# Queries and keys of one attention layer kept dimension by dimension over four heads, and copied through DRAM in that order

## What is computed

```python
qkv = (x1 @ mat_qkv_w.T + qkv_bias).reshape(B, L, 3, H, hd)      # B=16, L=256, H=16, hd=16
q, k, v = [jnp.transpose(qkv[:, :, i], (0, 2, 1, 3)) for i in range(3)]
q = _l2norm(q) * sm
k = _l2norm(k)
scores = jnp.einsum('bhqd,bhkd->bhqk', q, k)
probs = jax.nn.softmax(scores, axis=-1)
o = jnp.einsum('bhqk,bhkd->bhqd', probs, v)
```

## Time and profile before

| what | value |
|---|---|
| median of 3 runs | 795.8 us (793.74 to 796.53) |
| the profiled execution's own time | 793.83 us |
| its span, first to last instruction | 792.0 us |
| mean granted TensorE clock | 0.976 of full |
| PE busy | 731.9 us, 92% of the span |
| DVE busy | 498.2 us, 63% |
| DMA packets | 83096, 79.65 MB |

### The profile page before, as it was taken

One profiled execution on the slowest core, in us unless ns is written; L12 is line 12 of the kernel. 1 busy time (PEld: TensorE's weight loads), 2 busy tenths in 40 slices (PEclk: granted clock), 3 DMA queues, 4 the chain that ended last, 5 costly groups with the idle time before them and its releaser, 6 DMA issues.

```text
span 792.0 us, 15017 instructions
## 1 busy us (share of the span) xinstructions
PE 731.9 (92%) x4708; PEld 521.5 (66%) x4708; DVE 498.2 (63%) x1037; ACT 443.1 (56%) x733; POOL 326.1 (41%) x563
## 2 busy tenths in 40 slices
PE   4789999999996689999999999998889999999997
PEld 2477788888873345555555555555548888888885
DVE  2168999989999357767676767666425444444432
ACT  0335555555553266666666666666546555556553
POOL 1024655655653445555555555555442302222200
PEclk9999999999999599999999999999989999999999
DMA  8831333333311777776667767666500000000001
GB/s 239 292 98 37 111 94 115 115 94 113 103 32 40 126 133 149 148 147 150 146 147 146 147 147 147 146 147 155 125 14 1 22 19 14 27 27 28 14 27 40
DMA packets 83096, 79.65 MB, mean 101 GB/s; under 512 B 22942, under 2 KB 71710, under 8 KB 83054
## 3 DMA queue, kind: packets, MB, share of 16 engines
q1 hardware_dynamic: 81726, 78.95, 41.6%
q10 hardware_dynamic: 1328, 0.16, 0.1%
HBM read 57.13 MB, written 21.66 MB: 99 GB/s over the span
## 4 chain that ended last, share of the span: by engine, by line
PE 79%; ACT 6%; DVE 6%; issue 3%; DMA 1%; POOL 1%; ACTq 0%; SPq 0%; DVEq 0%; POOLq 0%
PE ps L1703 11%; PE ps L1717 11%; PE ps L1521 7%; PE ps L1439 7%; PE ps L1596 6%; PE ps L1582 6%; PE ps L1634 4%; PE ps L1531 4%; ACT probsT L928 4%; PE ps L1412 4%; PE ps L1430 4%; PE ps L1459 4%; PE ps L1470 3%; PE ps L1615 2%; PE ps L1548 1%
## 5 line engine op out<-in xcount | busy, mean ns | idle before, releaser
L928 ACT ACTIVATE probsT<-ps 128x1024 f32<-128x1024 f32 x128 | 130.5, 1019 | 29.8 <-PE ps L1582 29.5
L1331 DVE TENSOR_TENSOR hidden_low<-hidden,hidden_high 128x512 fp32r<-128x512 f32 x64 | 46.1, 721 | 115.0 <-ACT hidden_high L1024 67.1
L1021 ACT ACTIVATE hidden<-ps,b_fc 128x512 f32<-128x512 f32 x64 | 44.1, 689 | 73.5 <-PE ps L1703 72.5
L1582 PEld LDWEIGHTS ps<-q_stack,k_stack 49*128 49x128 f32 x512 | 39.0, 188 | 65.3 <-ACT probsT L928 35.3
L1582 PE MATMUL ps<-q_stack,k_stack 49*128 49x256 f32 x512 | 65.5, 335 | 11.9 <-ACT probsT L928 6.8
L1596 PE MATMUL ps<-probsT,v_ones 128*32 128x256 f32 x1024 | 69.2, 388 | 5.0 <-ACT probsT L928 4.8
L713 POOL TENSOR_TENSOR scores<-scores,row_max 128x640 f32<-128x640 f32 x32 | 42.4, 1324 | 76.2 <-DVE row_max L1060 76.2
L1225 DVE TENSOR_REDUCE neg_max<-ps 128x4 bf16<-128x344 f32 x128 | 59.5, 506 | 19.6 <-PE ps L1548 19.6
L1521 PE MATMUL ps<-w_qkv,x1T 128*128 128x512 f32 x128 | 65.3, 634 | 0.0
L1439 PE MATMUL ps<-x_res,w_q 128*128 (+1 forms) x256 | 63.7, 394 | 0.0
L1439 PEld LDWEIGHTS ps<-x_res,w_q 128*128 128x128 f32 x256 | 47.4, 194 | 11.1 <-issue 5.5
(11 more groups left out here) (181 smaller groups left out, 1714.2 us busy)
## 6 DMA issues: line engine op xcount, KB each, us to landing
parts_dram<-part_pairs SPq DMA_DIRECT2D x64, 256.0 KB
q_stack<-parts_dram SPq DMA_DIRECT2D x96, 128.0 KB, 5.3
k_stack<-parts_dram SPq DMA_DIRECT2D x96, 128.0 KB, 6.0
adj<-in_adj SPq DMA_DIRECT2D x16, 440.0 KB, 3.4
xT<-in_xT SPq DMA_DIRECT2D x16, 256.0 KB, 2.7
x_res<-in_x SPq DMA_DIRECT2D x16, 256.0 KB, 3.4
x_in<-in_x SPq DMA_DIRECT2D x16, 256.0 KB, 2.8
gate_rows<-rows_dram SPq DMA_DIRECT2D x16, 256.0 KB, 7.0
```

Source lines behind the costliest of these rows:

```text
L928: nc.scalar.activation(probsT[:, s % 4, :], ps[:, COLS:COLS + 2, :].rearrange("p a n -> p (a n)"), ACT.Exp).then_inc(exp_made, 1)
L1021: nc.scalar.activation(hidden[:, s % RAW, :], ps[:, FC1[s % FC1_BANKS], :], ACT.Gelu, bias=b_fc1[:, m:m + 1]).then_inc(gelu_made, 1)
L1331: nc.vector.tensor_tensor(hidden_parts[1][:, s % H_SLOTS, :], hidden[:, s % RAW, :], hidden_parts[0][:, s % H_SLOTS, :], ALU.subtract).the ...
L1582: mm = nc.tensor.matmul(ps[:, COLS + j, kt * N:(kt + 1) * N], k_stack[at, par, s, kt * P:(kt + 1) * P], q_stack[at, par, s, :], start=True ...
```

## The change

Within each of queries and keys the columns of SBUF are ordered by group of four heads, then dimension, then head (`g d a`, a = 4), where they were ordered by head, then dimension. PSUM, bias and weights keep the old order, so `take_qk` reads run by run and writes single elements 16 bytes apart. The sum of squares reads with the same step. `unit_qk` reads and writes in the new order, with the reciprocal roots of four heads repeated over the 16 dimensions. After the transposes a partition is (group of 4 heads, dimension, head), `parts_dram` holds [queries or keys, high or low, c, partition, token], and a dimension's four heads lie one behind the other in DRAM.

The mask `row_head` (1/3 where the partition's head is column a) follows: it is now a sum over the identity's columns, made by DVE in setup, where POOL made it from `head_of_row`.

```diff
-                    nc.gpsimd.tensor_tensor(row_head[:], head_of_row[:, 0:4], head_of_row[:, 4:8], ALU.add).then_inc(chain, 1)
-                    pool.wait_ge(chain, 5)
-                    nc.gpsimd.tensor_scalar(row_head[:], row_head[:], 1.0 / 3.0, 0.0, ALU.mult, ALU.add).then_inc(consts_set, 1)
...
+                    dve.wait_ge(consts_set, 5)
+                    nc.vector.tensor_reduce(row_head[:], ident[:].rearrange("p (q a) -> p a q", a=HT // 2), AX_X, ALU.add).then_inc(row_heads, 1)
+                    dve.wait_ge(row_heads, 1)
+                    nc.vector.tensor_scalar(row_head[:], row_head[:], 1.0 / 3.0, None, ALU.mult).then_inc(row_heads, 1)
...
-    parts_dram = nc.dram_tensor("parts_dram", (2, HT, 2, HD, C2 * N), F32, kind="Internal").ap()
+    parts_dram = nc.dram_tensor("parts_dram", (2, 2, C2, P, N), F32, kind="Internal").ap()
...
+        def store(par, w, part):
+            return sp.dma_start(parts_dram[w, part].rearrange("c p n -> p c n"), parts[:, par, w, part].bitcast(F32).rearrange("p (c n) -> p c n", c=C2))
...
-                sp.dma_start(parts_dram[w, :, 0], parts[:, par, w, 0].bitcast(F32)).then_inc(parts_out, 16)
+                store(par, w, 0).then_inc(parts_out, 16)
...
-                sp.dma_start(parts_dram[w, :, 1], parts[:, par, w, 1].bitcast(F32)).then_inc(low_out, 16)
+                store(par, w, 1).then_inc(low_out, 16)
...
-                sp.dma_start(stack[at:at + SLOT, par].bitcast(F32), parts_dram[w, :, part, :, c * N:(c + 1) * N].rearrange("h d n -> d h n")
+                sp.dma_start(stack[at:at + SLOT, par].bitcast(F32).rearrange("d (j a) n -> d j (a n)", j=2),
+                             parts_dram[w, part, c].rearrange("(j d a) n -> d j (a n)", j=2, d=HD)
                              ).then_inc(stack_in, 16)
...
-            nc.vector.tensor_tensor(qk[:, tt, :], ps[:, qk_bank(f, tt), :], bias_qk[:], ALU.add).then_inc(qk_out, 1)
+            by_head = "p (g a d) -> p g a d"
+            nc.vector.tensor_tensor(qk[:, tt, :].rearrange("p (g d a) -> p g a d", d=HD, a=4), ps[:, qk_bank(f, tt), :].rearrange(by_head, d=HD, a=4),
+                                    bias_qk[:].rearrange(by_head, d=HD, a=4), ALU.add).then_inc(qk_out, 1)
...
-            nc.vector.tensor_reduce(sum_sq[:, tt * 2 * H:(tt + 1) * 2 * H], squares[:, tt].rearrange("p (h d) -> p h d", d=HD), AX_X,
+            nc.vector.tensor_reduce(sum_sq[:, tt * 2 * H:(tt + 1) * 2 * H], squares[:, tt].rearrange("p (g d a) -> p g a d", d=HD, a=4), AX_X,
                                     ALU.add).then_inc(ss_made, 1)
...
-            nc.vector.tensor_tensor(qkn[:].rearrange("p t (h d) -> p (t h) d", d=HD), qk[:].rearrange("p t (h d) -> p (t h) d", d=HD),
-                                    root[0][:].unsqueeze(2).broadcast_to([P, HH, HD]), ALU.mult).then_inc(qkn_made, 1)
+            rows = "p t (g d a) -> p (t g) d a"
+            nc.vector.tensor_tensor(qkn[:].rearrange(rows, d=HD, a=4), qk[:].rearrange(rows, d=HD, a=4),
+                                    root[0][:].rearrange("p (g a) -> p g a", a=4).unsqueeze(2).broadcast_to([P, HH // 4, HD, 4]), ALU.mult).then_inc(qkn_made, 1)
```

More of the change, by code:

```diff
@@ L191, in build @@
                  cond_out, sum20_mm, nz_made, cond20_made, feat20_mm, feat20_made, kv_mm, kv_out,
-                 chain, clamped, place_clamped, place_exp, v_rows_mm, v_rows_out) = sems(
+                 chain, row_heads, clamped, place_clamped, place_exp, v_rows_mm, v_rows_out) = sems(
                     setup, "consts_set", "first_in", "kv_in", "small_in", "exp_made", "sig_made",
                     "silu_made", "cond_mm", "cond_out", "sum20_mm", "nz_made", "cond20_made",
-                    "feat20_mm", "feat20_made", "kv_mm", "kv_out", "setup_chain", "clamped",
+                    "feat20_mm", "feat20_made", "kv_mm", "kv_out", "setup_chain", "row_heads", "clamped",
                     "place_clamped", "place_exp", "v_rows_mm", "v_rows_out")
```

## The result

The changed kernel takes 805.7 us (median of 4 runs, 804.64 to 806.15), the kernel before 795.1 us beside it (4 runs, 793.74 to 796.53). The ratio is 1.0126, 95% interval 1.0102 to 1.0149: slower by 10.6 us. The prediction was 807, with 791.5 to 822 as its range. The profiled execution took 806.15 us, its span is 804.4.

What follows compares the result with a forecast made beforehand. PE, busy for 92% of the span, was taken to bound the kernel. Turns 11.5 plus start 2.6 minus earlier fetches 3.0 gave +11.1 us: 804.9 on the profiled execution, 807 against the median, range 791.5 to 822.

Steps and rivals of the forecast that it cites:

- The price of a hop: DVE's take_qk and sum_squares, elements 16 bytes apart: 0.32 us more an operation, at 0.6 ns a hop from L1243.
- The turn: Attention turn: four slower DVE operations make the division 1.03 us later, PE slips 0.62; 0.82 a turn, 11.5 us over 14.
- the predicted wait for the division: In the turns, PE would newly wait at L1627 for DVE's division, some 0.6 us.
- `unit_qk`: DVE in a turn: 0.41 us later after PE's slip, paid every second turn, 0.2 on average; its new form costs nothing.
- The stores: Attention start, 256 pieces of 1 KB a store: landing in 2.1 to 2.8 us, fetches some 2.6 us sooner.
- The gain at the start: First scores of the attention: the maxima row lands sooner, saving 2.7 to 3.4 us, taken as 3.0, once.
- The fetches: Fetches as 32 pieces of 4 KB instead of 128 of 1 KB: no gain, rate still near 137 GB/s.
- The start under the strides: Batches 0 and 1, before the maxima row: eight slower DVE operations at 0.32 us make it 2.6 us later.
- The sum: Whole kernel: 11.5 + 2.6 - 3.0 = +11.1 us on the profiled execution's 793.8.
- Setup: Two new small DVE operations of about 0.2 us each, hidden in front of L292's 7.04 us wait, cost nothing.

Runs made afterwards that it cites:

- The probe: Kernel before plus sixteen kinds of VectorE operation on 512 fp32 elements a partition, each twice, in setup, for their durations only; 814.5 us in one run.
- the squaring later: Changed kernel with ACT's squaring of a turn's slots 1 and 2 behind that slot's exponentials instead of ahead of them; 808.8 us, ratio 1.0187.
- the sums alone: Changed kernel with only sum_squares hopping and take_qk writing contiguously, for times only; 797.9 us, ratio 1.0035 to the kernel before.
- flat operations: Changed kernel with take_qk and sum_squares contiguous as before, transfers, unit_qk and mask still changed, for times only; 792.0 us, ratio 0.9955.
- the stores alone: Kernel before with only the DRAM buffer changed, so stores go as 128 rows of 2 KB instead of 8 x 16; 791.6 us, ratio 0.9960.

## Why the prediction was right, point by point

- **The price of a hop.** Predicted 0.32 us an operation, from 10 ns over the 16 hops of L1243; measured 0.39. The size is nearly right, partly by luck, since the reason behind it isn't: the same price holds for steps of 4, 8 and 16 words and falls to nothing at 2 words and for pairs, so it isn't "so much a hop". The Trainium skill, "Vector Engine (DVE) Microarchitecture Reference", section "Measured stream behaviour on trn2", asks for adjacent words in runs of two and gives 1.71 to 1.73 ns against 1.05 for one hopping side, an estimate of +0.34 us for 512 elements. The probe agrees within 0.05 us for one side, and pairs are free as it says. It differs for single elements at a step of 2 words, which here were free, and for its small steps on the destination (2.50 ns), where 4 to 16 words here cost no more than 0.39 us.
- **The turn.** Predicted +0.82, measured +0.83; over 14 turns 11.6 us. The size rests on a wrong step: "New waits of PE in the turns, for the division at L1627, of some 0.6 us". PE waits for the exponentials instead. I had followed DVE's queue down to the division and never asked who takes take_qk's result first. It is ACT, whose squaring stands ahead of the exponentials. The sum came out since all of these are links of one chain: with the squaring later, the predicted wait for the division appears (9.0 us in 12 turns). That the two sizes agree to 0.01 is luck in part: with the measured price the same steps give 4 x 0.39 - 0.25 - 0.41 + 0.2 = 1.10, so the price, too low by 0.07 four times over, hid that the steps behind it ask for 0.27 too much.
- **`unit_qk`.** Predicted as paid in full every second turn, 0.2 on average. It rose from 2.0 to 4.0 us in 12 turns, 0.17 each. The alternation shows in the turns of the sums alone. Its own new form costs nothing, as predicted (1773 ns on average with flat operations, 1775 before). What makes every second turn the tight one is POOL. The end of the roots releases both `unit_qk` and POOL's bias addition (L782). In each of the twelve turns, before and after, exactly one of the two is about 1.1 us longer than it is elsewhere: `unit_qk` 2.35 beside an addition of 1.28, or `unit_qk` 1.23 at 387.36 beside this one:

```profile
387.39 2.34 POOL L782 TENSOR_TENSOR x_res<-x_res,gate_rows 128x512 f32 x1
```

  In the changed kernel, of the first eleven turns, the five with the longer `unit_qk` last 20.79 to 20.87 us and the six with the longer addition 20.36 to 20.40 (before: 19.76 to 19.84, and 19.71). So the price of the strides in a turn, 1.0 or 0.7 us, also hangs on which of two instructions, released together, is the longer one. Their order was not changed in any run.
- **The stores.** Predicted landing 2.1 to 2.8 us, measured 2.7. Fetches predicted 2.6 us sooner; the stores alone give 3.14. The gain at the start was 3.0 in the sum and 3.43 by the scores of that run. The granted clock, to which most of a further 1.85 up to the first projection is due, has no term in the sum. The 0.40 and 115 GB/s that the prediction read for the old stores are too low: the window of 6 us begins with about one in which nothing moves yet (see the last section).
- **The fetches.** Predicted no gain from pieces of 4 KB; measured 140 GB/s against 137, and the kernels with 1 KB and with 4 KB pieces take 791.6 and 792.0 us. The rule on ports in the Trainium skill ("SBUF — State Buffer", "Door 1: The DMA port swizzle") led one to think so, though the figure it gives for partitions 0 to 15, 104 GB/s, is below what these transfers to two halves reach. No run put the rows on other partitions, so what holds the fetches near 140 GB/s is not shown.
- **The start under the strides.** Predicted +2.6 us for eight operations in a row. The changed kernel's scores start 0.9 us later than those of flat operations relative to the feature matmul (273.23 - 74.09 = 199.14 against 271.78 - 73.53 = 198.25). Most of the delay had fallen into the wait for the maxima row and the other idle time ahead of it. The rest came behind the scores: up to the first projection the changed kernel takes 36.59 us where flat operations take 32.82. Of the 3.77 more, 1.66 is idle time of PE, two turns' worth of the growth. The other 2.11 is busy time for the same 230 matmuls (32.49 against 30.38), at a granted clock of 0.90 and not 0.95. So the term comes to 0.9 + 2.1 = 3.0 us, near the 2.6, but most of it by way of the clock, which the prediction doesn't have. What lowered the clock there was not followed.
- **The sum.** +11.1 predicted. Between the two profiled spans, 792.0 and 804.4 us, the parts as measured are +2.93 up to the feature matmul, which isn't of the change; -2.59 from there to the first scores (199.14 against 201.73); +1.91 to the first projection; +9.96 in twelve turns; +0.19 behind them: 12.4. Without the shift that is 9.5, where the sum had 11.1. The medians give +10.6 and an interval of about 8 to 12, so the two don't contradict each other.
- **Setup.** The two new operations on DVE are hidden: the wait that they stand in front of, 7.04 us in the earlier trace rows, is there as before with 6.82 us.

## What to carry to other kernels

When a layout makes an engine hop, look at how many words lie together and how far single ones are apart: here two heads side by side instead of four kept the idea and lost the price. When an operation gets longer, list everyone who reads its result, and what stands behind that reader in its own queue, before following the operation's own queue. And a transfer's shape can matter more than the length of its pieces: ask which of its dimensions is the outermost.

## What the runs showed of the hardware

**The store's outermost count.** While nothing but the first four stores moves, the same 128 rows of 2 KB go at 177 GB/s and a share of 0.52 as 8 x 16 rows, and at 381 GB/s and 1.02 as 128 rows (busy time by stretch; before, then stores alone):

```profile
254.00:257.00 3.00, 0.32 (x2) 0.12 (x2) 2.90 (x9) 0.00 (x0) 2.09 (x3) 0.72 0.52 177
```

```profile
254.00:256.00 2.00, 0.00 (x0) 0.00 (x0) 2.00 (x5) 0.64 (x2) 1.92 (x6) 1.00 1.02 381
```

The share is halved, as if eight of the 16 engines worked. The Trainium skill has the rule for that: in "DMA: Bandwidth & Descriptors", section "Why a DMA increments its semaphore by 16 and not by 1", the number of engines for a transfer is the largest up to 16 that divides the slowest dimension of both sides, so 8 for 8 x 16 x 512. The runs agree with it, but no view counted the engines of a single transfer, and no run kept the outermost 8 with high and low parts standing apart.

**The kernel with the stores alone** beats both kernels (791.6 against 795.1 and 805.7 us), by the order of the dimensions of a DRAM buffer.

**What stays open.** With the squaring later, the strided operations themselves grew to 1176 and 1127 ns on average, from 1079 and 1066; the sums alone took 1119. Between 300 and 460 us of the kernel with the squaring later, no POOL instruction runs beside the longer ones. What they met was not found.
